# Expert rows and gates turned by VectorE's block transposes instead of products of TensorE

## The reference

```
gate  = softmax(x @ gate_w + gate_b)          # 8 experts, the top 2 of each row are kept
h1    = relu(x  @ w1[e] + b1[e])
h2    = relu(h1 @ w2[e] + b2[e])
y     = (h2 @ w3[e] + b3[e]) * gate[row, e]   # then relu, and a sum over the rows of a tile
```

## Time and profile before

| | us |
|---|---|
| runs shown | 1007.7, 1007.0, 1005.17 |
| median | 1007.0 |
| profiled execution, span | 1003.7 |
| PE busy | 934.0 (93%) |
| VectorE busy | 429.3 (43%) |
| ScalarE busy | 346.5 (35%) |
| GpSimd busy | 250.9 (25%) |
| stage "experts", first transpose to last sums turned | 437.9 to 671.4 |

### The profile page before, as it was taken

How to read it: one execution, slowest core, us unless ns; L and a number is a source line. 1 busy time by engine, 2 the same in 40 slices (tenths; PEclk the granted TensorE clock), 3 DMA queues, 4 the chain that set the end, 5 groups by cost and what they waited for, 6 DMA issues and landing times. The chain is left out here.

```text
span 1003.7 us, 19227 instructions
## 1 busy us (share of the span) xinstructions
PE 934.0 (93%) x7747; PEld 757.2 (75%) x7747; DVE 429.3 (43%) x994; ACT 346.5 (35%) x886; POOL 250.9 (25%) x306
## 2 busy tenths in 40 slices
PE   5999999989998889999999999999889899999994
PEld 5977776676775644789999999987765578999532
DVE  2973454224442647002112132135267630656576
ACT  2322323245552124122222233324276611122374
POOL 5452111023554306000000010004065403000275
PEclk9999999999999979899999999997969998999996
DMA  9994000245622807259999888700040032971001
GB/s 254 382 331 127 2 2 2 98 152 203 238 120 95 309 7 254 55 181 386 358 383 313 284 269 283 254 29 28 4 153 3 2 119 78 321 247 66 1 15 51
DMA packets 72456, 162.01 MB, mean 161 GB/s; under 512 B 4132, under 2 KB 5685, under 8 KB 70321
## 3 DMA queue, kind: packets, MB, share of 16 engines
q1 hardware_dynamic: 70048, 156.54, 45.8%
q0 software_dynamic: 2320, 4.25, 1.4%
HBM read 128.81 MB, written 31.97 MB: 160 GB/s over the span
## 5 line engine op out<-in xcount | busy, mean ns | idle before, releaser
L2113 PE MATMUL ps<-ffn_h,ffn_w 128*128 128x128 f32 x1280 | 149.1, 275 | 0.0
L2113 PEld LDWEIGHTS ps<-ffn_h,ffn_w 128*128 128x128 f32 x1280 | 145.9, 192 | 0.0
L2113 PE MATMUL ps<-ffn_xh,ffn_w 128*128 128x128 f32 x640 | 74.9, 275 | 0.3 <-ACT ffn_xh L2147 0.3
L2203 DVE TENSOR_SCALAR ffn_h<-ps,tile_bias 128x128 f32<-128x128 f32 x80 | 22.5, 345 | 122.4 <-PE ps L2113 122.4
L2113 PEld LDWEIGHTS ps<-ffn_xh,ffn_w 128*128 128x128 f32 x640 | 73.1, 192 | 0.9 <-issue 0.9
L1418 POOL TENSOR_TENSOR ctx_low<-shelf,ctx_high 128x1024 fp32r<-128x1024 f32 (+2 forms) x24 | 43.0, 1819 | 65.4 <-PE ps L1283 33.7
L2161 ACT ACTIVATE ffn_y<-ffn_y 128x128 f32<-128x128 f32 x80 | 23.7, 298 | 73.9 <-DVE ffn_y L2219 73.9
L1526 PE MATMUL ps<-x_qT,ctx_ct 128*128 128x100 f32 (+1 forms) x384 | 46.4, 284 | 2.3 <-PEq L137 2.0
L1526 PEld LDWEIGHTS ps<-x_qT,ctx_ct 128*128 128x128 f32 (+1 forms) x384 | 45.0, 197 | 3.7 <-issue 3.2
L2219 DVE SCALAR_TENSOR_TENSOR ffn_y<-ps,tile_bias,ffn_gate_row 128x128 f32<-128x128 f32 x80 | 22.6, 344 | 58.0 <-PE ps L2113 57.9
L2834 POOL TENSOR_TENSOR att_e<-att_e,decay 100x400 f32<-100x400 f32 x32 | 32.7, 1033 | 46.1 <-DVE att_e L2685 46.1
(11 more groups left out here) (469 smaller groups left out, 2096.8 us busy)
## 6 DMA issues: line engine op xcount, KB each, us to landing
ffn_w<-in_L_ffn_w_dram SPq DMA_DIRECT2D x60, 1024.0 KB, 6.0
shelf<-in_ctx_dram SPq DMA_DIRECT2D x12, 1280.0 KB
expert_rows<-nothing SPq DMA_DIRECT2D x1, 14820.0 KB, 49.6
context_turned<-ctx_ct SPq DMA_DIRECT2D x8, 1444.0 KB, 7.9
ctx_ct<-context_turned SPq DMA_DIRECT2D x8, 1444.0 KB, 12.5
ctx_lent<-in_ctx_dram SPq DMA_DIRECT2D x4, 1280.0 KB
rows_own<-expert_rows SPq DMA_DIRECT2D x8, 260.0 KB, 3.0
x_wo<-in_L_xattn_Wo_dram SPq DMA_DIRECT2D x1, 2048.0 KB, 9.5
```

The lines of the kernel that those rows point to most:

```text
L2113: mm = nc.tensor.matmul(acc(n)[:, m, :], w[:, n % SLOTS, k, m * P:(m + 1) * P], into[l][:, i % 2, k, :], start=k == 0, stop=k == C - 1, sk ...
L2203: nc.vector.tensor_scalar(h2[:, i % 2, m, :], acc(n)[:, m, :], bsel[:, m, i, 1:2], 0.0, ALU.add, ALU.max).then_inc(h2_kept, 1)
```

## The change

Rows are turned by VectorE. Its transpose works in blocks of 32x32, each inside its own 32 partitions, so it cannot move a value from one group of 32 partitions to another. The gather does that part: the features are cut in four groups of 128 (f), and group f of all 128 rows goes to partitions 32f to 32f+31, row i*32 + r on partition 32f + r, block i. One transpose of 128x512 then leaves on partition 32f + d, block k, the feature f*128 + k*32 + d of each row. The first layer's weight is loaded in the same order of features, in four loads of 32 partitions each. The gates go, likewise in four parts per tile, to every group of partitions in a buffer of their own, `gates_raw`; one transpose of a broadcast column then spreads them. TensorE's and ScalarE's steps for both are gone. Three tiles are gathered ahead instead of six (`EARLY`), later ones behind every second weight, the six loads for the next layer behind them.

```diff
@@ -1672,10 +1672,14 @@
-        expert_w = [g[f"L0_ffn_w{i}"].rearrange("e (c p) o -> p e c o", p=P) for i in (1, 2, 3)]
+        first_w = g["L0_ffn_w1"].rearrange("e (f k d) o -> f d e k o", f=HPC, k=C)
+        group = lambda f: slice(f * HD, (f + 1) * HD)
+        expert_w = [g[f"L0_ffn_w{i}"].rearrange("e (c p) o -> p e c o", p=P) for i in (2, 3)]
...
@@ -1684,8 +1688,13 @@
             i, l = units[n]
-            sp.dma_start(w[:, n % SLOTS, :, :], expert_w[l][:, bass.ds(expert, 1)].rearrange("p a c o -> p (a c) o")
-                         ).then_inc(w_landed[n % SLOTS], 16)
+            if l == 0:
+                for f in range(HPC):
+                    sp.dma_start(w[group(f), n % SLOTS, :, :], first_w[f, :, bass.ds(expert, 1)].rearrange("d a k o -> d (a k) o")
+                                 ).then_inc(w_landed[n % SLOTS], 16)
+            else:
+                sp.dma_start(w[:, n % SLOTS, :, :], expert_w[l - 1][:, bass.ds(expert, 1)].rearrange("p a c o -> p (a c) o")
+                             ).then_inc(w_landed[n % SLOTS], 16)
...
-        AHEAD = 6
+        AHEAD, EARLY = 6, 3
...
         def gather(sp, i):
             row = sp.value_load(table[0:1, 1, i:i + 1], min_val=0, max_val=SPARE)
-            sp.dma_start(rows_of_tile(i), rows_dram[bass.ds(row, P), :]).then_inc(gathered[i], 16)
+            here = rows_dram[bass.ds(row, P), :]
+            for f in range(HPC):
+                sp.dma_start(rows_of_tile(i)[group(f), 0:D].rearrange("r (i d) -> r i d", d=P),
+                             here[:, f * P:(f + 1) * P].rearrange("(i r) d -> r i d", r=HD)).then_inc(gathered[i], 16)
+                sp.dma_start(gates_raw[group(f), i],
+                             here[:, D:XW].rearrange("(i r) e -> r i e", r=HD)).then_inc(gathered_gates[i], 16)
...
-                for i in range(AHEAD):
+                for i in range(EARLY):
                     gather(sp, i)
...
                     load_unit(sp, n, expert)
                     if n >= SLOTS - 1 and more < MT:
-                        gather(sp, more)
-                        more += 1
+                        if n % 2:
+                            gather(sp, more)
+                            more += 1
                     elif more == MT and last:
...
             def _(pe):
-                def turn(i):
-                    pe.wait_ge(gathered[i], 16)
-                    if i >= 2:
-                        pe.wait_ge(kept, i - 1)
-                    for c in range(C):
-                        mm = nc.tensor.transpose(ps[:, 3 + i % 2, c * P:(c + 1) * P], rows_of_tile(i)[:, c * P:(c + 1) * P],
-                                                 ident[:, :])
-                    mm.then_inc(turned, 1)
-
-                def spread_gate(i):
...
                         for k in range(C):
                             if l and m == 0:
                                 pe.wait_ge((h1_kept, h2_kept)[l - 1], C * i + k + 1)
+                            rhs = xh[:, i % 2, :, k, :] if l == 0 else into[l][:, i % 2, k, :]
                             mm = nc.tensor.matmul(acc(n)[:, m, :], w[:, n % SLOTS, k, m * P:(m + 1) * P],
-                                                  into[l][:, i % 2, k, :], start=k == 0, stop=k == C - 1,
+                                                  rhs, start=k == 0, stop=k == C - 1,
                                                   skip_group_check=True)
...
             def _(act):
-                def keep(i):
-                    act.wait_ge(turned, i + 1)
-                    if i >= 2:
-                        unit_made(act, i - 2, 0)
-                    nc.scalar.activation(xh[:, i % 2, :, :], ps[:, 3 + i % 2, :].rearrange("p (c t) -> p c t", c=C),
-                                         ACT.Identity).then_inc(kept, 1)
-
...
             def _(dve):
+                def turn(i):
+
+                    dve.wait_ge(gathered[i], 16 * HPC)
+                    if i >= 2:
+                        unit_made(dve, i - 2, 0)
+                    nc.vector.transpose(xh[:, i % 2].rearrange("p i k r -> p (i k r)"), rows_of_tile(i)[:, 0:D]).then_inc(kept, 1)
+
...
+                def spread_gate(i):
+
+                    dve.wait_ge(gate_col, i + 1)
+                    if i >= 2:
+                        dve.wait_ge(weighed, C * (i - 1))
+                    nc.vector.transpose(gate_row[:, i % 2, :], gate[:, i % 2, :].unsqueeze(2).to_broadcast([P, HPC, HD])
+                                        ).then_inc(rows_kept, 1)
+
...
+                turn(0)
                 for n, (i, l) in enumerate(units):
+                    if n + 1 < len(units) and units[n + 1][1] == 0:
+                        turn(units[n + 1][0])
                     if l == 0:
                         gate_of(i)
                     elif l == 1:
+                        spread_gate(i)
                         second_layer(n, i)
                     elif l == NL - 1:
                         weigh(n, i)
...
                 for i in range(MT):
-                    pool.wait_ge(gathered[i], 16)
+                    pool.wait_ge(gathered_gates[i], 16 * HPC)
                     if i >= 2:
                         pool.wait_ge(gate_col, i - 1)
-                    nc.gpsimd.tensor_tensor(gates[:, i % 2, :], rows_of_tile(i)[:, D:XW], mine[:, i, :],
+                    nc.gpsimd.tensor_tensor(gates[:, i % 2], gates_raw[:, i], mine[:, i:i + 1, :].to_broadcast([P, HPC, E]),
                                             ALU.mult).then_inc(gated, 1)
```

More of the change, by code:

```diff
@@ L1678, in program @@
         w_landed = [sem(f"ffn_landed{s}") for s in range(SLOTS)]
+        parts_of = lambda n: HPC if units[n][1] == 0 else 1
+        landed_by = [16 * sum(parts_of(m) for m in range(n % SLOTS, n + 1, SLOTS)) for n in range(len(units))]
         def expert_of(sp, i):
@@ L1777, in program @@
         fold_bank = lambda n: ps[:, (7, 0, 1)[n % 3], :]
-        gathered = [sem(f"rows_gathered{i}") for i in range(MT)]
+        gathered, gathered_gates = ([sem(f"{what}_gathered{i}") for i in range(MT)] for what in ("rows", "gates"))
         def gather(sp, i):
             row = sp.value_load(table[0:1, 1, i:i + 1], min_val=0, max_val=SPARE)
-            sp.dma_start(rows_of_tile(i), rows_dram[bass.ds(row, P), :]).then_inc(gathered[i], 16)
+            here = rows_dram[bass.ds(row, P), :]
[4 more added lines that the diff above has]
+                             here[:, D:XW].rearrange("(i r) e -> r i e", r=HD)).then_inc(gathered_gates[i], 16)
         with nc.Block() as block:
@@ L2209, in gate_of @@
                     if i >= 2:
[L2210 to L2211 removed]
+                        dve.wait_ge(rows_kept, i - 1)
+                    nc.vector.tensor_reduce(gate[:, i % 2, :], gates[:, i % 2], AX.X, ALU.add).then_inc(gate_col, 1)
+                def spread_gate(i):
[4 more added lines that the diff above has]
+                                        ).then_inc(rows_kept, 1)
                 def weigh(n, i):
```

38 lines of the change are left out of this document (9 added, 29 removed).

## The result

The changed kernel takes 1062.1 us, median of 4 runs (1056.1 to 1065.7), beside 1006.1 us (1005.0 to 1007.7) for the kernel before: a ratio of 1.055, interval 1.051 to 1.059. The forecast was 1018 with a range of 993 to 1036. The sign and the kind of bound came out as forecast; the size did not. The profiled execution has a span of 1060.7 us.

The account below looks back on a forecast made before the run. The prediction had TensorE pacing the expert stage before and DMA loads pacing it after: 23.7 us of weight waits less 13.1 us saved on TensorE, net +10.6 on 1007.0, about 1018; range 993 to 1036.

Parts of the forecast that it names:

- the kind of bound: Expert stage: DMA-paced instead of TensorE-paced, PE idle for ffn_w some 24 us at full DMA share; chance 0.33.
- TensorE's 13.1 us: Expert stage: row transposes (7.9 us), gate products (4.6) and start (0.6) leave TensorE, 13.1 us gained.
- VectorE hidden: VectorE's two new transposes per tile, 0.78 us (at most 2.28) and 0.3, stay hidden behind TensorE.
- SyncE: SyncE's issues while gathers last: 10.7 us per tile against TensorE's 10.7, fitting with no margin except the six slots.
- rival 3: SyncE's issues pace the stage: 1012 at 0.5 us per issue, 1032 at 0.6; chance 0.13.
- Rivals 1 and 2: 1: TensorE still paces, 32-partition loads at 2.7 us, 993.9, chance 0.27; 2: first weight 3.7 to 4.1, 1004 to 1010, 0.12.
- The first weight's 4.6 us: DMA time of a first-layer weight in four 32-partition loads, taken at the slow window's 227 GB/s: 4.6 us.
- the gather's 1.2: DMA time of one tile's row gather in 512-byte pieces, 0.27 MB at 227 GB/s: 1.2 us.
- Rival 5: Half rate: four 32-partition loads share the paths of half the partitions, 5.4 us per first weight, 1029; chance 0.15.
- the sum: DMA queue up to unit 43's weight: 172.7 us of first weights, other weights, gathers and late loads; TensorE waits 23.7 us.
- After that 10.2 us per tile is under 10.7 and nothing waits: Expert stage after unit 43 and the late loads: DMA needs 10.2 us per tile against TensorE's 10.7, no waits.
- ScalarE's late loads, nothing added: ScalarE's wait for the next layer's six loads, landing near 616 us, leaves 4 us for 4 us of work: nothing added.

Follow-up runs that it names:

- rows_one_load: rows_cut_early with a tile's rows in one load of 128 partitions (values in the wrong places), gates still in four: 991.8 us, ratio 0.988.
- before_w_groups: The kernel before, only the first-layer weight in four loads of 32 adjacent partitions: 1057.1 us, ratio 1.056.
- after_w_whole: The changed kernel with the first-layer weight again in one load of 128 partitions (values differ): 1009.4 us, ratio 1.004.
- rows_cut_early: The changed kernel with whole first-layer weights, GpSimd reordering x before the scatter so values fit: 1006.9 us, ratio 1.001.
- draining: The changed kernel with SyncE waiting, ahead of every sixth unit's weight, until all earlier weights have landed: 1047.3 us, ratio 1.043.

## Why the prediction was wrong

- **TensorE's 13.1 us: right.** rows_one_load is 14.0 us faster than the kernel before.
- **VectorE hidden: right.** 0.70 and 0.31 us; one wait of TensorE for it, 1.8 us, at the start.
- **SyncE: right for this kernel.** PE waits while the share is full, so rival 3 is out.
- **The kind of bound: right.** PE waits for `ffn_w` at full share. Rivals 1 and 2 are out; both rested on narrow loads being cheap.
- **The first weight's 4.6 us: right alone** (4.64), and so are the gather's 1.2, 0.7 + 0.5, and the gates' 0.3. Rival 5's reason fits the pattern, since loads of 64 adjacent partitions are as slow as those of 32 (228 and 224), but its price of 5.4 us is too high for loads alone and its 1029 too low for the kernel. The 189 GB/s of the Trainium skill's page on SBUF is below all that was measured for such loads alone, 202 to 248.
- **The step that failed is the sum: it takes for granted that prices of loads on their own add up in the kernel.** It laid 172.7 us of DMA time end to end, some 50.4 MB at 292 GB/s. From 448 to 628 us the stage moved 231 to 248. At 240 the same bytes take 210 us, 37 more: 61 us of waits instead of 24, and so +48 instead of +10.6; measured are +56. Whole loads beside narrow ones were priced at 2.8 us, and the loads together moved less than these prices give: before_w_groups and after_w_whole put 51 to 56 us on the first weights, where the sum had 14 x 1.8 = 25. With whole first weights the sum has no wait at all, 993.9 as in rival 1; rows_one_load took 991.8, but rows_cut_early, with narrow gathers, 1006.9.
- **"After that 10.2 us per tile is under 10.7 and nothing waits": wrong** for the same reason. The waits go on while the rate stays at 231 to 265.
- **A term was missing:** a wait costs more than its length. Eight units behind waits ran partly at the lower clock, 13.5 us more, and stopping and starting again at 30 waits took 8.1 us.
- **ScalarE's late loads, nothing added: right**, though they came at 659 us and not near 616. Its wait is 21.5 us, and no wait of TensorE in the stage is put down to ScalarE.

What stays open: how the products first disturb the DMA engines, why the changed kernel is at 232 GB/s before its loads are far out of step, why narrow gathers cost 2.3 us in rows_cut_early (2.37 MB per two units at 306 GB/s is 7.7 us, less 5.4 for two whole weights) and 1.2 alone, and the rest of the loss that draining did not give back.

## What to carry to other kernels

Where the DMA engines are full, the price of a narrower load has to be taken with its neighbours and with the engines computing: this one was priced right alone, at 25 us more in all, and cost 51 to 56. Before data are laid out for groups of 32 adjacent partitions, try the loads alone in the old kernel, as before_w_groups did; it gives the answer without the rest of the change. Of a change with several parts, time each alone: here the gates were worth keeping.

## What the hardware showed that was not expected

- Four loads of every fourth partition run as fast as one whole load (387 GB/s; in the kernel 1.000); of 32 adjacent ones 224, of 64 adjacent 228, groups taken in the order 0, 2, 1, 3 248.
- A mixed stream at 306 GB/s, once disturbed by products, sinks to 250 with nothing else running; a wait for all loads at every sixth unit keeps 306 between the waits, with the products running.
- Of waits of the same 1.86 us, one left TensorE at full clock, and behind the other a unit took 5.47 us instead of 3.84.
- Loads whose outermost count is 4 move 102 GB/s at a share of 0.26, with 5 semaphore events each instead of 16.
- VectorE's float32 transpose in 32x32 blocks: 0.70 us for 128x512, 0.31 for 128x128.
